# Expert rows gathered one every second step, each combined five steps after its gather

## The reference

```python
xn = _layernorm(x, axis=-1)
x = x + _L0_attn_ref(xn, W_qkv, W_o) + _L0_ffn_ref(xn, router_w, router_b, w1, w2)
# attention: 16 heads of 64, rotary on half of each head, causal softmax, projection W_o
# experts:
probs = softmax(xn @ router_w + router_b)            # 8 experts and a skip
top_v, top_i = top_k(probs, 2)
h = gelu(einsum('btd,edf->ebtf', xn, w1)); y = einsum('ebtf,efd->ebtd', h, w2)
out = sum over the two chosen of gate * y  (or gate * xn for the skip)
```

## Time and profile before

| | us |
|---|---|
| median of 3 runs | 1568.7 |
| lowest and highest | 1566.03, 1572.05 |
| the profiled execution, its own time | 1575.69 |
| its span, from first to last instruction | 1574.0 |
| PE busy | 1302.8 (83%) |
| DVE busy | 1155.5 (73%) |
| ACT busy | 1130.1 (72%) |
| POOL busy | 849.2 (54%) |

### The profile page before, as it was taken

The page is one execution under the profiler, slowest core; times in us unless marked ns, Lnnn a source line. Parts: engine busy times, 40 slices in busy tenths (PEclk is TensorE's granted clock), DMA queues, the critical chain, the costliest instruction groups (busy, mean ns, idle before and its releaser), DMA issues.

```text
span 1574.0 us, 46446 instructions
## 1 busy us (share of the span) xinstructions
PE 1302.8 (83%) x15156; PEld 1005.9 (64%) x15157; DVE 1155.5 (73%) x4018; ACT 1130.1 (72%) x3606; POOL 849.2 (54%) x1194
## 2 busy tenths in 40 slices
PE   2416999999898999877999997888888888888878
PEld 1304676677676666656898895666666666666656
DVE  5787777776777777655777777777777778778776
ACT  6415787788877887775788887677777777777766
POOL 3244777777777777661000004666666666666655
PEclk9657999999999999997999999999999999999999
DMA  9621433333333333341232322333333333333330
GB/s 287 188 50 38 89 75 71 69 70 79 88 71 69 79 88 70 69 122 46 84 87 83 87 85 53 81 73 75 75 86 77 74 79 76 79 81 77 75 75 25
DMA packets 115831, 130.12 MB, mean 83 GB/s; under 512 B 11568, under 2 KB 75312, under 8 KB 115376
## 3 DMA queue, kind: packets, MB, share of 16 engines
q1 hardware_dynamic: 107056, 110.26, 29.5%
q0 software_dynamic: 8576, 17.33, 3.9%
HBM read 28.85 MB, written 31.59 MB: 38 GB/s over the span
## 4 chain that ended last, share of the span: by engine, by line
DMA 25%; PE 22%; POOL 18%; DVE 17%; issue 13%; ACT 4%; SPq 0%; POOLq 0%; DVEq 0%; ACTq 0%
DMA sorted_x_dram<-stage,slots 16%; DMA stage<-sorted_y_dram,slots 7%; PE bank L1087 5%; PE bank L1088 5%; PE bank L1089 5%; POOL arena L454 4%; DVE arena L947 4%; POOL arena L453 3%; POOL sorted_x_dram L493 3%; POOL arena L478 2%; DVE arena L910 2%; ACT probs L640 2%; POOL stage L484 2%; PE bank L1158 2%; DVE arena L909 1%
## 5 line engine op out<-in xcount | busy, mean ns | idle before, releaser
L640 ACT ACTIVATE probs<-arena,neg_max 128x128 f32<-128x128 f32 (+1 forms) x1024 | 455.5, 449 | 235.1 <-DVE neg_max L947 223.2
L947 DVE CUSTOM_DVE_ANT_0 arena<-bank,causal 128x128 f32<-128x128 f32 (+1 forms) x1024 | 302.8, 350 | 25.4 <-PE bank L1158 23.6
L1168 PE MATMUL bank<-ident,probs 128*128 128x128 f32 x1536 | 248.9, 277 | 69.3 <-DVE probsT L969 56.5
L503 POOL DMA_INDIRECT stage<-sorted_y_dram,slots x128 | 126.9, 991 | 260.4 <-DMA sorted_y_dram<-stage 238.0
L1168 PEld LDWEIGHTS bank<-ident,probs 128*128 128x128 f32 x1536 | 183.1, 143 | 107.7 <-ACT probs L640 70.2
L1195 PE MATMUL bank<-probsT,arena 128*64 128x256 f32 x1024 | 226.6, 415 | 19.0 <-ACT probsT L623 18.4
L1158 PE MATMUL bank<-arena 64*128 64x128 f16 (+1 forms) x3072 | 175.0, 248 | 28.0 <-DVE neg_max L947 25.8
L640 ACT ACTIVATION_READ_ACCUMULATOR probs<-arena,neg_max 128x1 f32 x1024 | 197.4, 193 | 0.0
L493 POOL DMA_INDIRECT sorted_x_dram<-stage,slots x128 | 131.1, 1024 | 115.1 <-DMA sorted_x_dram<-stage,slots 92.7
L623 ACT ACTIVATE probsT<-bank 128x384 f32<-128x384 f32 x384 | 186.1, 485 | 7.0 <-PE bank L1168 6.5
L473 POOL TENSOR_TENSOR arena<-o_whole,arena 128x256 f16<-128x256 f32 x256 | 173.0, 676 | 21.2
(11 more groups left out here) (152 smaller groups left out, 3297.9 us busy)
## 6 DMA issues: line engine op xcount, KB each, us to landing
arena<-arena SPq DMA_DIRECT2D x256, 256.0 KB
arena<-sorted_x_dram SPq DMA_DIRECT2D x72, 128.0 KB, 2.2
sorted_y_dram<-stage SPq DMA_DIRECT2D x72, 128.0 KB, 1.8
sorted_x_dram<-arena SPq DMA_DIRECT2D x3, 2304.0 KB, 17.8
arena<-experts_dram SPq DMA_DIRECT2D x8, 512.0 KB, 5.4
out_dram<-acc SPq DMA_DIRECT2D x32, 128.0 KB
sorted_x_dram<-arena SPq DMA_DIRECT2D x1, 2368.0 KB, 18.7
sorted_x_dram<-stage,slots POOLq DMA_INDIRECT x128, 2.3
```

The lines of the kernel that those rows point to most:

```text
L640: last = nc.scalar.activation(probs[:, s % 4, at:at + w], masked[:, s % 4, at:at + w], ACT.Exp, bias=neg_max[:, s % 4, t:t + 1], scale=-1. ...
L947: last = nc.vector.tensor_tensor_reduce(out=masked[:, (s + i) % 4, at:at + w], in0=SC[i][:, at:at + w], in1=causal[:, at:at + w], scale=1. ...
L1168: last = nc.tensor.transpose(TP[s % 2][:, k * P:(k + 1) * P], probs[:, s % 4, k * P:(k + 1) * P], ident[:])
```

## The change

The gathers of a sample are issued at every odd step. Combine k comes five steps behind gather k: the first five at steps 6, 8, 10, 12 and 14 of the sample, and k = 5, 6 and 7 at steps 0, 2 and 4 of the next one. For the last sample these three stand in `rest_of`, behind `o_scale` of the seventh pair of heads and ahead of that of the eighth. All combines move from odd steps (one of the eight, k = 5, was at an even one) to even steps, so each now stands between the even and the odd half of DVE's pair of steps. Number and size of the gathers and combines stay the same, as do the four buffers.

```diff
-GATHER_AT = [1, 3, 5, 7, 9, 10, 11, 13]
-COMBINE_AT = [3, 5, 7, 9, 11, 12, 13, 15]
+GATHER_AT = [1, 3, 5, 7, 9, 11, 13, 15]
+COMBINE_AT = [6, 8, 10, 12, 14, 16, 18, 20]
@@ beside(b, s, at), last lines
                 if b >= MID and s in COMBINE_AT:
                     combine(b, COMBINE_AT.index(s))
+                elif b > MID and s + H in COMBINE_AT:
+                    combine(b - 1, COMBINE_AT.index(s + H))
@@ rest_of(b, at)
                 o_scale(8 * b + 6, 6)
                 if at == TURN:
                     mix(b)
+                else:
+                    for k in range(5, 8):
+                        combine(b, k)
                 o_scale(8 * b + 7, 7)
```

## The result

The changed kernel takes 1506.9 us (median of 4 runs, 1505.4 to 1510.1), the kernel before 1568.9 us beside it (4 runs): a ratio of 0.961, 95% interval 0.958 to 0.963. The profiled execution took 1505.9 us, with a span of 1504.1.

A forecast was written before the change was run, and what follows sets the result against it. DVE's terms summed to -84 us, but the prediction took PE to bound the latter half next: at 94% busy a sample takes 35.2 us, 16 x 3.5 = 56 less 1 gained, giving 1514 us, range 1492 to 1540.

The forecast's parts named there:

- The waits, -67.2 us: Latter half, DVE ahead of the combines: all idle time waiting for gathered rows should go, 67.2 us less.
- a stall of DVE lengthens a sample one for one: Latter half: twelve samples less waits and combine surplus come to 33.1 us each, so each DVE stall counts in full.
- The budget of 7.6 us: Tightest case, gather 0 to its new combine: 7.6 us without the stalls between, against a longest landing of 5.62 us.
- The old surplus and the new, -25.5 and +19: Combines' time beyond 0.34 us each: the old 25.5 us goes; four places a sample behind invert cost 0.3 us each, +19.
- The gap ahead of L915, -11: Four combines a sample ahead of rest_low fill DVE's idle time for ACT: between 0 and -22 us, half taken.
- PE is what is late next.: Latter half: PE's 33.1 us of work at 94% busy makes a sample 35.2 us, 55 us gained in all.
- DVE's account of 33.4: Latter half: DVE's terms sum to -84 us, a sample of 33.4 us; as rival 1, 1485 us, chance 0.17.
- The queues and buffers, nothing: POOL and SP queues and stage buffers: no cost, 1.4 us as nearest row above; delayed q_rope_low has a late reader.
- The end, +1: Last sample: combines 5 to 7 now stand ahead of the last o_scale, about +1 us.
- the combines collide with o_split: Rival 4, latter half: each combine held for both o_split instructions, +44 us, 1613; decides from 0.72 us mean hold; chance 0.05.
- The rule of the Trainium skill: VectorE instructions with two SBUF inputs share a read interface with GpSimd's SBUF reads; alone it exposes all eight new places.

The follow-up runs named there:

- the two variants with the shortest samples: Changed kernel with L478 a step later in both halves, 1512.1 us; changed kernel with combines four steps behind and gathers at former steps, 1485.9 us.

## Why the prediction was right, and where it was not

The forecast of 1514 us and its range of 1492 to 1540 hold the measured 1506.9, and a latter sample of 34.8 us is close to the 35.2 forecast. The waits went as it said; that the sample stopped near 35 us was right for a reason that was wrong. The steps:

- **The waits, -67.2 us.** Right: 0.5 us is left. That distance does it is shown by the run with distance and old gathers (0.958) against the one with spacing and two steps (1.000). That a stall of DVE lengthens a sample one for one is not: 3.9 us of waits went and 1.2 us of surplus came, which by that rule makes a sample 2.7 us shorter, and it became 3.9 shorter; among the variants a microsecond of surplus is worth about 0.7.
- **The budget of 7.6 us.** Right, and generous: at three steps, 5.8 us in the case that I read, the landings cost only 2.3 us of waits.
- **The old surplus and the new, -25.5 and +19.** For the combines it came out at 52.7 - 43.5 = 9.2 us left, not 19: of the four places behind invert only the one of step 8 met L473 in nearly every sample (0.77 us). This term was too high, but the account was incomplete: it priced the hold for the moved instruction alone. With the samples shorter, L961 and L921 came to stand beside POOL's instructions and grew by 21.2 + 8.6 = 29.8 us. (With the new gathers but samples as long as before, in the run with two steps, L961 took 12.2 us in twelve samples, as before.) In sum the surplus rose from 2.7 to 3.9 us a sample.
- **The gap ahead of L915, -11.** The gap did shrink, from 31.8 to 15.7 us in twelve samples, about 21 over sixteen. That it is a gain of the new place was wrong: at odd steps the gap stays and the kernel is faster.
- **"PE is what is late next."** This is the step that failed. I took PE's work to be 33.1 us a sample, from a stretch with stalls and the clock at 0.97; in the changed kernel it is 31.3, and PE is busy for 90% of the sample, not for the 93 to 95% that I gave as the sign. DVE is still what the others wait for, together with POOL's hold on it, and 0.3 us more of PE a sample left its length as it was. Whether PE becomes the limit later is open: the two variants with the shortest samples run it at 95% through the latter half, about the 94% of the expert stage that I took for a ceiling, and no run added work to PE there. The floor that I charged for PE, 1.8 us a sample over DVE's account of 33.4, happens to be near the 1.4 us by which the sample really exceeds that account. That was luck.
- **The queues and buffers, nothing.** Right: POOL waited 1.4 us for combines, as before. But the reason given for q_rope_low, that its reader has time, holds only for one gather's 0.98 us; with L478 a step later the stacking comes late, which shows as 6.6 to 10.3 us of ACT's waits in twelve samples.
- **The end, +1.** The three combines take 1.50 us between the last two o_scales, which start 1495.25 - 1493.49 = 1.76 us apart, where they were 0.91 apart: +0.85.
- **A slip in the reading.** The stretch of twelve samples ends with a first combine, at 1466.46, as it begins with the end of one. It holds 96 combines; the 97th only touches its edge, so the surplus in it is 20.9 us and not 20.6. Nothing else changes.
- **The rivals.** That the combines collide with o_split into a loss did not happen; the mean hold was 412 - 340 = 72 ns a combine, a tenth of the 0.72 us at which it decides. The rule of the Trainium skill behind it ("SBUF — State Buffer", "Who interferes with whom") was nevertheless the one to follow further. The page also names tensor_scalar among the VectorE instructions that can contend with GpSimd, in its two-port modes and where its operands allow these. The trace agrees so far: L961, a TENSOR_SCALAR with a single tensor input, in SBUF, was held to 1.31 us. In which mode it ran the trace does not tell.

Not settled: why a shorter combine gives back only half of its time, which chain between DVE, ACT and PE makes the common 31 us, and whether PE is the limit of the fastest variants. No run took those apart.

## What to carry to other kernels

A landing that an in-order engine waits for cost at least its whole wait here, where the others follow that engine; put the reader as many steps behind as the landing needs and no more, and move only the reader. Before moving work to another place on VectorE, look at what GpSimd does then, for that instruction and for the ones behind it: the hold moves to the next one that can be held (here L888, L961, L963 or L921). Take an engine's floor from a stretch at the clock that it will have and without the stalls that are to go.

## What the runs showed of the hardware

POOL held DVE before its own reading instruction had begun, and the issue of an indirect DMA alone did not. In the kernel before, 25 combines began while POOL issued a gather. Eleven of them, 0.26 to 0.52 us behind the start of the issue, lasted 1.8 to 2.07 us, through the rest of the issue and the whole of the next instruction, L478, which followed 0.02 us behind it (1118.22 against 1117.96). Two more had L478 behind the issue but began 0.21 and 0.23 us into it, and took 0.35 us. The other twelve began 0.06 to 0.91 us into the issue, and POOL had nothing ready behind it; all took 0.34 or 0.35 us. One of the two latest, on DVE and then on POOL with the instruction that came next:

```profile
1399.94 0.35 DVE L888 SCALAR_TENSOR_TENSOR acc<-stage,gates,acc 128x128 f32<-128x128 f32 x1
```

```profile
1399.03 0.98 POOL L503 DMA_INDIRECT stage<-sorted_y_dram,slots  x1
1402.26 0.40 POOL L471 CAST arena<-o_whole 128x256 f16<-128x256 f32 x1 [2.25 <-DVE o_whole L974]
```

So what held a combine was L478 waiting ready behind the issue, from some quarter of a microsecond into it. The step-4 L961 of the changed kernel fits: it began 0.89 us into the issue and ended with L478. No run was made for this reading; the one with L478 a step later, in which the L961 of twelve samples fell from 32.4 to 11.3 us, agrees with it.

Also unexpected: PE's busy time for the same work in twelve samples fell from 397.4 to 375.5 us as its stalls went, with the granted clock rising from 0.97 to 1.00 between them. Before, the clock was at 0.50, the level of 1.2 GHz, in eight stretches of 3.4 us; it accounts for 0.03 x 397 = 12 of these 22 us. The rest is not slower matmuls: outside those stretches a matmul lasts 264 ns on average before, and 265 after. Busy time counts the overlap of two of them once, and it comes to 85.1 ns a matmul there against 82.4 after, so after the change more of them overlap. A busy time read from a stretch with stalls is too long a floor.
